# Masked layer of a four-layer graph kernel: two blocks of its first chunk evicted by VectorE, its join cut into pieces of 64 columns, four masks made ahead, and five places in the order changed

## What is computed

```python
# layer 0: h = relu(layernorm(x))
Ax = adj @ h;  x = x + 1 - 0.1*h - 0.01*sum(h*Ax, axis=1)
# layer 1: two hops
for k in range(2):  h = tanh(concat([adj @ h, h], axis=1) @ W[k])
# layer 2 (the masked layer)
mask = (adj != 0)
rank = cumsum(mask, axis=1);  deg = rank[:, -1:];  k = minimum(deg, 100)
pos  = rank - (deg - k)
w    = mask * where(pos > 0, 0.5 ** (k - pos), 0.0)
out  = w @ (h @ weight) + bias
# layer 3
u = tanh(concat([h, t]) @ W1 + b1) @ W2 + b2
out = u + adj @ (h @ B.T) - rowsum(adj) * (h @ B.T)
```

## Time and profile before

| | |
|---|---|
| median of three runs (lowest to highest) | 700.03 us (698.61 to 701.37) |
| the profiled execution, and its span | 700.7 us, 698.9 us |
| busy: PE, VectorE, ScalarE, GpSimd | 668.3, 469.6, 192.5, 114.2 us |
| moved by DMA | 256.51 MB, mean 367 GB/s |
| L1B's last product ends, about | 426.5 us |
| L2's first load is issued | 429.06 us |
| L3's first product starts | 562.14 us |
| last eviction of the sums starts | 694.67 us |

### The profile page before, as it was taken

How to read it: one execution, slowest core, us unless ns; L and a number is a source line. 1 busy time by engine, 2 the same in 40 slices (tenths; PEclk the granted TensorE clock), 3 DMA queues, 4 the chain that set the end, 5 groups by cost and what they waited for, 6 DMA issues and landing times.

```text
span 698.9 us, 10418 instructions
## 1 busy us (share of the span) xinstructions
PE 668.3 (96%) x3811; PEld 270.2 (39%) x3824; DVE 469.6 (67%) x813; ACT 192.5 (28%) x296; POOL 114.2 (16%) x132
## 2 busy tenths in 40 slices
PE   3999999999999999999999998899999999999997
PEld 1434433334433333333344443444444443333332
DVE  7777767777899999996888888899989810000000
ACT  1101111011111001101111116899998811111111
POOL 4110011110200000001222223222332211211111
PEclk9999999999999999999999999999999999999999
DMA  8999999998589999959999983999999479999992
GB/s 347 422 410 411 413 412 409 418 414 335 190 329 388 420 422 419 415 206 402 384 406 420 419 368 134 362 378 408 414 414 412 191 263 341 417 415 418 417 419 98
DMA packets 42098, 256.51 MB, mean 367 GB/s; under 512 B 5120, under 2 KB 11264, under 8 KB 11840
## 3 DMA queue, kind: packets, MB, share of 16 engines
q1 hardware_dynamic: 38712, 252.85, 89.6%
q10 hardware_dynamic: 3336, 3.00, 1.5%
HBM read 252.28 MB, written 3.54 MB: 366 GB/s over the span
## 4 chain that ended last, share of the span: by engine, by line
PE 53%; DMA 20%; DVE 19%; POOL 4%; issue 3%; ACT 0%; SPq 0%; DVEq 0%; ACTq 0%; POOLq 0%
PE accA L1373 37%; DMA cache<-adj_blocks 10%; DVE uS L1111 8%; DMA land<-adj_blocks 6%; PE accA L1424 4%; PE work L1408 4%; DVE uS L1155 3%; POOL rstd L762 2%; DMA rows_transposed<-rowsT 2%; PE work L1391 1%; PE work L1336 1%; POOL tS L772 1%; PE accA L1342 1%; PE work L1267 1%; PE work L1304 1%
## 5 line engine op out<-in xcount | busy, mean ns | idle before, releaser
L1373 PE MATMUL accA<-land,X 128*64 128x512 f32 x1568 | 374.1, 598 | 13.6 <-DVE X L1197 11.3
L1373 PEld LDWEIGHTS accA<-land,X 128*64 128x64 f32 x1568 | 110.6, 137 | 193.7 <-issue 166.9
L1155 DVE TENSOR_SCALAR uS<-land 128x1024 bf16<-128x1024 f32 (+1 forms) x196 | 134.5, 730 | 30.1 <-DMA land<-adj_blocks 28.4
L1111 DVE TENSOR_TENSOR uS<-uS,land 128x512 f32<-128x512 f32 x178 | 125.2, 704 | 9.6
L1373 PE MATMUL accA<-cache,X 128*64 128x512 f32 x480 | 120.1, 598 | 2.6 <-DMA cache<-adj_blocks 2.6
L591 ACT ACTIVATE wS<-work 128x1024 uint16<-128x1024 f32 x114 | 109.2, 1037 | 8.8 <-PE work L1408 8.7
L769 POOL TENSOR_TENSOR hS<-tS 128x256 f32<-128x256 f32 x24 | 23.5, 978 | 400.5 <-DVE tS L979 400.5
L1097 DVE TENSOR_TENSOR zS<-uS,work 128x256 f32<-128x256 f32 x8 | 3.4, 421 | 123.1 <-PE work L1267 106.9
L1408 PE MATMUL work<-uS,triA 128*128 128x512 bf16 x248 | 74.4, 380 | 2.2 <-DVE uS L1155 1.8
L1424 PE MATMUL accA<-wS,X 128*128 128x512 bf16 x251 | 74.7, 379 | 0.3
L850 ACT ACTIVATE accS<-accA 128x512 f32<-128x512 f32 x32 | 19.1, 598 | 177.3 <-PE accA L1373 165.5
(11 more groups left out here) (109 smaller groups left out, 417.4 us busy)
## 6 DMA issues: line engine op xcount, KB each, us to landing
land<-adj_blocks SPq DMA_DIRECT2D x221, 1024.0 KB, 10.3
cache<-adj_blocks SPq DMA_DIRECT2D x15, 1024.0 KB, 16.7
xin<-x_rows ACTq DMA_DIRECT2D x8, 128.0 KB, 7.6
out_rows<-zS ACTq DMA_DIRECT2D x8, 128.0 KB, 6.9
uS<-counts ACTq DMA_DIRECT2D x60, 4.0 KB
x_rows<-zS SPq DMA_DIRECT2D x7, 128.0 KB, 11.4
rows_transposed<-rowsT SPq DMA_DIRECT2D x7, 128.0 KB, 8.6
wS<-rows_transposed SPq DMA_DIRECT2D x7, 128.0 KB, 8.5
```

Source lines behind the costliest of these rows:

```text
L1111: nc.vector.tensor_tensor(total, total, of[:, i * W:(i + 1) * W], ALU.add)\
L1155: nc.vector.tensor_scalar(masks(p, c, b)[0:rows, :], block_of(p, c, b)[0:rows, :], 0.0, None, ALU.not_equal)\
L1373: last = nc.tensor.matmul(accA[k * D:(k + 1) * D, c % 2, :], tile(X[p % 2], TQ * q + k), of[:, k * W:(k + 1) * W], start=(b == 0), stop=(b ...
```

## The change

- `evac_on_dve(0)` is (8, 13) rather than empty: VectorE evicts two of the first chunk's sixteen blocks.
- The join in L2 is done as elsewhere, in eight products of 64 result partitions, after block 4; before, it was four products of 128 after blocks 4 and 5.
- `MASKS_AHEAD`: the masks of L2's blocks 0 to 3 are made in L1B's last chunk, after the adds of its blocks 10, 12, 13 and 14.
- At L2's start VectorE's list is put in another order, the last fold comes in two halves behind the sum and the variance of the layer norm, and its scratch is `zS`; the join of L1B's last chunk stands behind block 1 of L2 rather than ahead of block 0, and the stages that follow it come one or two blocks earlier.
- In L1A "added" and "tanh" stand one block earlier; in L1B stage 5 stands one block later.
- `keep_rows` leaves SyncE's queue for ScalarE's, right behind the transpose's eviction.
- The last chunk of L3 is evicted, joined, added and stored in two halves.

```diff
 def evac_on_dve(c):
-    return (3, 13) if c else ()
+    return (3, 13) if c else (8, 13)
+MASKS_AHEAD = {10: 0, 12: 1, 13: 2, 14: 3}
...
-STAGES_L1A = {1: 2, "added": 4, "tanh": 6, "hop": 8, "hopped": 10}
-STAGES_L2 = {0: 2, "join0": 4, "join1": 5, 4: 5, 5: 7, 6: 10, 7: 13, 8: 15}
-STAGES_L1B = {1: 3, "added": 5, "tanh": 6, 3: 7, 4: 8, 5: 10, "turn": 12, "turned": 13, 6: 14, 8: 15}
+STAGES_L1A = {1: 2, "added": 3, "tanh": 5, "hop": 8, "hopped": 10}
+STAGES_L2 = {0: 2, "join": 4, 4: 5, 5: 7, 6: 10, 7: 13, 8: 15}
+STAGES_L1B = {1: 3, "added": 5, "tanh": 6, 3: 7, 4: 8, 5: 11, "turn": 12, "turned": 13, 6: 14, 8: 15}
...
-         L2: {"tanh": 0, 4: 0, 5: 2, "turn": 8, "turned": 9, 6: 10, 7: 10, 8: 11,
-              "row sums": 14},
+         L2: {"tanh": 0, "join": 1, 5: 1, "turn": 7, "turned": 7, 6: 9, 8: 9,
+              "row sums": 12},
...
-                if issued["keep"] < NC - 2 and g >= PAIRS * (issued["keep"] + 2) + 2:
-                    keep_rows(issued["keep"])
-                    issued["keep"] += 1
...
                     rows_transposed(p, c)
+                    if p == L2 and c < NC - 1:
+                        act.wait_ge(tr_evac, tr_no(p, c) + 1)
+                        act.dma_start(hT_d[ch(p, c)], rowsT[:, :]).then_inc(hT_out, 16)
...
+                if at == "last sums":
+                    act.wait_ge(intra_done, c + 1)
+                    act.wait_ge(swept, sweep_no(p, c) + 1)
+                    act.wait_ge(nat_done, nat_no(p, c))
+                    for h in range(2):
+                        nc.scalar.activation(accS[:, h * CH:(h + 1) * CH], accA[:, c % 2, h * CH:(h + 1) * CH], ACT.Copy)\
+                            .then_inc(acc_evac, 1)
...
                 if p == L2 and c == 0:
-                    for b in range(2):
-                        mask(p, c, b)
-                    fold_totals(L1B, NC - 1)
-                    nc.vector.tensor_tensor(part_sums, part_sums, more_sums, ALU.add).then_inc(folded, 1)
+                    mask(p, c, len(MASKS_AHEAD))
                     epilogue("added", before)
-                    for b in range(2, 4):
+                    for b in range(len(MASKS_AHEAD) + 1, LEAD):
                         mask(p, c, b)
                     epilogue(3, before)
-                    for b in range(4, LEAD):
-                        mask(p, c, b)
+                    fold_totals(L1B, NC - 1, halves=(0,))
+                    epilogue(4, before)
+                    fold_totals(L1B, NC - 1, halves=(1,))
+                    nc.vector.tensor_tensor(part_sums, part_sums, more_sums, ALU.add).then_inc(folded, 1)
```

More of the change, by code:

```diff
@@ L341, in last_stages @@
 def last_stages(before):
-    return [(k, before) for k in SUM_STAGES]
+    return [("last " + k, before) for k in SUM_STAGES]
 def sweep_steps(step, finish):
@@ L679, in _ @@
             LEFT_ROWS_AT = {NC - 3: 1, NC - 2: 3, NC - 1: 7}
-            issued = {"keep": 0, "left": 2, "left rows": NC - 3}
+            issued = {"left": 2, "left rows": NC - 3}
             def step(p, c, before, before2):
@@ L697, in step @@
                     after_masks(PAIRS * NC - 1)
-                    keep_rows(NC - 2)
                 if p == L0:
@@ L895, in epilogue @@
                                          bias=hbias[:, h:h + 1]).then_inc(hidden_ready, 1)
+                if at == "last sums":
[5 more added lines that the diff above has]
+                            .then_inc(acc_evac, 1)
+                if at == "last store":
+                    for h in range(2):
+                        act.wait_ge(nat_evac, nat_no(p, c) + 1 + h)
+                        act.dma_start(last_half(chunk(out, ch(p, c)), h), last_half(zS, h)).then_inc(rows_out, 16)
                 if at == ("store" if p == L3 else 7) and p in rows_to and not rows_by_sync(p, c):
@@ L948, in finish @@
                     epilogue(k, e)
-                act.wait_ge(rows_out, 16 * 2 * NC)
+                act.wait_ge(rows_out, 16 * (2 * NC + 1))
             for g in range(1, PRO_GROUPS):
@@ L1091, in epilogue @@
                     side = sideS[:, (c % 2) * CH:(c % 2 + 1) * CH]
+                    if at == "last result":
+                        dve.wait_ge(side_ready, c + 1)
+                        rows_written()
+                        for h in range(2):
+                            dve.wait_ge(nat_done, nat_no(p, c) + 1 + h)
+                            nc.vector.tensor_tensor(last_half(zS, h), last_half(side, h), last_nat(h), ALU.add)\
+                                .then_inc(nat_evac, 1)
                     if at == "result":
@@ L1120, in main @@
                             weights_out(dve, nc.vector, c, k)
+                if (p, c) == (L1B, NC - 1) and b in MASKS_AHEAD:
+                    mask(L2, 0, MASKS_AHEAD[b])
                 if p == L2 and NQ * c + b + LEAD < NQ * NC:
@@ L1124, in main, with fold_totals @@
                     weights_out(dve, nc.vector, c, b)
-            def fold_totals(p, c):
+            def fold_totals(p, c, halves=(0, 1)):
                 k = ch(p, c)
@@ L1435, in step @@
             def step(p, c, before, before2):
-                for k, e in early_stages(p, c, before, before2):
-                    epilogue(k, e)
                 s = NC * p + c
```

41 lines of the change are left out of this document (24 added, 17 removed).

## The result

The kernel after takes 701.53 us (median of 16 runs, 700.37 to 703.87) against 699.97 us of the kernel before, run beside it (16 runs, 698.55 to 703.35). The ratio is 1.0025, with a 95% interval of 1.0014 to 1.0035: slower by 1.6 us, which is within the 0.5% that the prediction called no change. The profiled execution spans 700.0 us (698.9 before).

The account below looks back on a forecast made before the run. L2's stream of loads, started by VectorE's last fold, was taken to bound the kernel. L3's start + 2.8, L1A - 0.2, tail - 0.3 make + 2.3 on the median 700.03: 702.3 us; 8-in-10 range 695.5 to 705.0.

Parts of the forecast that it names:

- the stream: L2's 43 loads of a pair of blocks each, 2.80 us a pair, taken to end last in L2.
- The order at L2's start: VectorE's new list at L2's start ends the fold at 433.3; first load at 433.6, 4.6 us later (2.5 to 5.5).
- L1A and L1B: "added" one block earlier in L1A and the norm behind adds in L1B: 0.2 us gained, bounds 0 and 0.9.
- within the stream's price: L1B's last chunk: a mask joins the adds, TensorE's transpose may be 0.2 late, counted as no extra cost.
- That idle time goes: L2's first chunk: earlier transpose and product remove TensorE's 1.57 us idle before 449.62, ahead of loads 1.5 to 4 us later.
- The 1.1 us given back: L2's first six loads catch up 1.1 of 2.7 us (bounds 0 and 2.7), so the last landing is 3.5 us later.
- at the same pace: L2's loads keep their pace, so the last landing moves with the first load, by 4.6 us.
- From the last landing to L3: VectorE's 0.69 us wait for the join goes: 7.9 becomes 7.2 us, L3 starts at 564.9, 2.8 later.
- The tail: L3's last chunk in halves, first eviction and join overlapping the second: 0.3 us gained, bounds 0 and 0.6.
- engines, not the stream: Rival: engines end last in L2, so their gains show: 5.3 us, 694.7, or 696.6 without the joins; chance 0.22.
- the larger loss: Rival: first load after 434, nothing given back, last landing 5 to 5.5 us later: 704.9; chance 0.20.
- The wash: Rival: first load only 2.5 us late, L3 starts within 1 us of before, 700; chance 0.58 together with the forecast.

Follow-up runs that it names:

- a_fold: The kernel after, with the last fold in one piece and first in VectorE's list of L2; ratio 0.9955 to the kernel before.
- b_late: The kernel before, with SyncE waiting for the mask of L2's block 7 before L2's first load; ratio 1.0082.
- b_l1: The kernel before, with only the new orders of L1A ("added", "tanh" one block earlier) and L1B (stage 5 one later); ratio 0.9973.
- a_left: The kernel after, with the last `later<-X` DMA issued on ScalarE's queue at block 12 of L2's first chunk; ratio 1.0002 to the kernel before.
- b_join: The kernel before, with only L2's join changed to eight products of 64 result partitions behind block 4; ratio 0.9970.
- b_spread: The kernel before, with rows of the counts 2 KB apart in DRAM, so each transfer goes as four 1 KB pieces; ratio 0.9987.
- f_left_spread: f_left with the counts also sent in four pieces of 1 KB; ratio 0.9915 to the kernel before, 693.89 us.
- f_left: a_fold with the last `later<-X` DMA also issued by ScalarE instead of SyncE; ratio 0.9964 to the kernel before.

## Why the prediction came out as it did

The forecast was + 2.3 us on the median, 702.3; it is + 1.6. The mechanism is confirmed: the fold stands late, the first load waits for it, and the stream passes the delay on (a_fold, b_late). But four terms were wrong, and they nearly cancelled; that the sum came within 0.7 us of the measured time is luck in part.

1. **The order at L2's start: right.** Counted from "added", the working had 5.0 us to the fold's end (428.3 to 433.3); it takes 4.6 (426.49 to 431.07). As a whole the order puts 4.3 us more between L1B's end and the fold's, and the text had 4.6. a_fold prices the fold's place at 4.9 us of the final time, a part of which is point 3.

2. **L1A and L1B: mis-sized, 0.2 for 1.9 us** (b_l1). The step that failed is "within the stream's price": the norm behind the adds was costed by what TensorE's transpose loses, and not by what VectorE wins. The working had filled the idle 1.81 us with a mask and two adds and so knew of it, but it took L1B's end, 426.78, as fixed. What VectorE wins, 1.5 us, can be had only where the fold follows the adds, as in the kernel before; in after the fold stands behind "added" and so behind L1B's end. There only a shorter L1B counts: 124.12 to 124.15 us in the seven traces with the masks ahead, 0.2 to 0.3 us less than in the old order. L1B's end came at 424.84 in the profiled run, and that is the most of the difference between the forecast first load, 433.6, and the 431.4 measured. But of these 1.94 us 0.85 is there at L0's end, which the change does not touch, 0.84 arises in L1A, where traces of one order differ by as much, and 0.25 in L1B: mostly scatter of single executions.

3. **TensorE's stalls: missing.** "That idle time goes" failed: the stall for `later<-X` grew from 1.57 to 2.37 us. The text brought forward the product that needs the DMA, and did not ask how the DMA stands in its queue: three unfinished loads ahead of it instead of two, 8.4 us to arrive. The second stall, for the counts that wait for the fold, isn't in the text at all, although it names this very DMA as the one that the fold releases; it looked at who queues behind it and not at who reads it. Both stalls lower TensorE's clock. The one for `later<-X` costs 1.6 us (a_left against after), by way of VectorE's eviction that waits for TensorE.

4. **The 1.1 us given back: none.** The stream took 125.5 us, 0.35 more than before; b_late and a_fold show 125.5 and 125.6 too, the latter without a wait for a small DMA. The step that failed is "at the same pace". The first six loads did catch up, by 3.2 us where the text gave back 1.1: in after the sixth lands 449.8 - 431.4 = 18.4 us after the first is issued, where it was 21.6 us and the text had 18.9 at best.

```profile
L756 SPq DMA_DIRECT2D land<-adj_blocks x1: 328/328/328, 439.2 to 439.2; - x1
...
DMA to landing us min/median/max: 10.6/10.6/10.6
```

But the other 37 then took 556.9 - 449.8 = 107.1 us, 2.89 each and not 2.80 (b_late 2.89, a_fold 2.87, a_left 2.84). Part of that is point 3: a_left's stream takes 123.8 us, 1.4 less than before's. Why the pace is lower in a_fold and b_late as well stays open.

5. **From the last landing to L3: - 0.7 forecast, - 1.0 measured; the step is only half of it.** VectorE's wait for the join does go, as b_join shows, but b_join keeps 7.7 us, since TensorE then ends last. The text took TensorE's own lag as nothing here and put `keep_rows` at "nothing on the sum"; that store's wait is the rival that fits the traces and was not tested.

6. **The tail: - 0.3, as forecast** (4.23 to 3.91 us).

The text also said that the join "is worth nothing here"; b_join gains 0.3% (0.9952 to 0.9987). Of its signs of being right, landing times of 15 us come from the load of 490.6 on, about the middle of L2, VectorE waits for loads seven times in L2 (4.9 us, where before had two, 1.4 us), and L3 starts at 563.8.

On the rivals: "engines, not the stream" was said to need slack in the stream which the text could not find. 3 us of it could be had, by an edit that is not in the change: the counts in small pieces. With that and the fold in front the kernel runs at 693.5 to 693.9 us, which is close to the 694.7 us worked out for that rival, but by another way, so the match proves nothing for it. The point of 434 for the larger loss was not reached by after. The wash had its first load (2.3 us late, for 2.5) but not its end: L3 starts 1.65 us later than before, not within 1.

## What to carry to other kernels

When a step is moved, follow every DMA that it releases, to the engine that reads it and not only to the queue that waits: here a 4 KB transfer stalled TensorE and lowered its clock. Place the step that opens the next stage's stream of loads before all work that can wait, and fill the waits ahead of that step: b_l1's table entries gained 1.9 us that way. Many small transfers that go out in one piece can lengthen a stream of large loads (here 3.0 to 3.3 us of 125); try them in several pieces. And read more than one trace before taking a starting time as fixed: L2's start differed by 1.8 us between traces of the same order.

## What the runs showed of the hardware

- One-piece DMAs of 4 KB, 60 of them in 120 us, lengthened a stream of 43 loads of 1 MB by 3.0 to 3.3 us (b_spread and before, f_left_spread and f_left), and four pieces of 1 KB each took that away. Cutting costs issue time on the queue: the one that SyncE issues for the counts took 0.22 us as one piece and 0.58 us in b_spread.
- A small DMA behind queued loads on the same queue needs 8.4 us in after from its issue at 441.37 until the product that waits for it starts, and some 4.3 us in before (445.32): three loads of 1 MB unfinished ahead of it in after, two in before.
- TensorE's granted clock fell to its lower level after idle times of 2.12 and 2.37 us (after), and in b_late after 5.6 us (0.58 of full in 449 to 454); it did not after 1.57 us in before. The cost in after: groups of two products 0.83 to 0.86 us apart rather than 0.43, in both stretches.
- GpSimd's small operations run slower while VectorE works than while it waits: 1.38 and 0.85 us (418.35 and 419.81 in after, VectorE with a mask and adds) against 1.01 and 0.61 us for the same two in the kernel before, where VectorE is idle. A step that fills VectorE's wait for GpSimd thus made GpSimd's two steps end later (2.3 us from first to last here, 1.7 in before); TensorE's wait for the result grew from 0.58 to 1.20 us.
